# Node update of a two-layer graph network: ring of seven x blocks, counts inverted once, scalings on ScalarE, biases as bf16 rows, 14 blocks a turn

## What is computed

```python
feat_in, feat_out = h @ W_in.T + b_in, h @ W_out.T + b_out
a = concatenate(seg_mean(feat_in[src], dst), seg_mean(feat_out[dst], src))   # sums / max(count, 1)
gi, gh = a @ w_ih.T + b_ih, h @ w_hh.T + b_hh
r, z = sigmoid(i_r + h_r), sigmoid(i_z + h_z)
n = tanh(i_n + r * h_n)
x = layernorm(x + (1 - z) * n + z * h)                                        # layer 0, h = x
m = relu(concatenate(x[src], x[dst], bond) @ W1 + b1) @ W2 + b2
x = layernorm(x + x + segment_sum(m * sigmoid(bond @ Wa + ba), src))          # layer 1
```

## Time and profile before

| | us |
|---|---|
| three runs: median (lowest, highest) | 23,088.97 (23,025.80, 23,107.62) |
| profiled execution, its own time | 23,050.08 |
| its span | 23,048.5 |
| busy in it: PE / DVE / ACT / POOL | 12,864.9 / 8,520.6 / 3,852.9 / 9,828.0 |
| mean granted clock of PE | 0.681 of full speed |

### The profile page before, as it was taken

One profiled execution on the slowest core, in us unless ns is written; L12 is line 12 of the kernel. 1 busy time (PEld: TensorE's weight loads), 2 busy tenths in 40 slices (PEclk: granted clock), 3 DMA queues, 4 the chain that ended last, 5 costly groups with the idle time before them and its releaser, 6 DMA issues. The chain is left out here.

```text
span 23048.5 us, 371307 instructions
## 1 busy us (share of the span) xinstructions
PE 12864.9 (56%) x76034; PEld 9943.0 (43%) x76035; DVE 8520.6 (37%) x33126; ACT 3852.9 (17%) x9613; POOL 9828.0 (43%) x10418
## 2 busy tenths in 40 slices
PE   3444443444444444445555556777777777777773
PEld 2222223333333333335555544555555555555552
DVE  4333343332333333335545544333333333333333
ACT  0000001111111111100000002233333333333331
POOL 2444444444444444444444420344444444444440
PEclk9655556666666666667777778677677777777775
DMA  6222222222222222234444430111111131111131
GB/s 231 35 35 35 37 42 56 69 68 68 68 69 68 69 68 68 68 84 113 114 113 114 114 73 15 43 44 44 45 44 45 44 44 45 45 45 45 44 44 30
DMA packets 3234314, 1465.86 MB, mean 64 GB/s; under 512 B 2388398, under 2 KB 3029362, under 8 KB 3233775
## 3 DMA queue, kind: packets, MB, share of 16 engines
q1 hardware_dynamic: 2794486, 548.09, 12.8%
q0 software_dynamic: 386304, 796.93, 12.7%
q10 hardware_dynamic: 53492, 120.52, 1.5%
HBM read 1108.06 MB, written 467.75 MB: 68 GB/s over the span
## 5 line engine op out<-in xcount | busy, mean ns | idle before, releaser
L1522 POOL DMA_INDIRECT ring<-q_rows,small x3556 | 3369.8, 948 | 4597.3 <-ACT ring L1616 3609.8
L1562 PE MATMUL bank<-w,ring 64*128 64x129 f32 x7112 | 2334.8, 420 | 2074.4 <-DVE ring L1476 1183.7
L1562 PEld LDWEIGHTS bank<-w,ring 64*128 64x128 f32 x7112 | 1450.0, 254 | 2754.8 <-issue 1323.8
L876 PE MATMUL bank<-ident_b,ring 128*128 128x128 bf16 x3332 | 489.1, 298 | 3578.9 <-DVE ring L825 2241.1
L698 POOL DMA_INDIRECT ring<-in_x,small x1664 | 1572.5, 945 | 1926.7 <-DVE small L595 1276.3
L1080 POOL DMA_INDIRECT ring<-in_x,small x1664 | 1572.1, 945 | 1889.4 <-DVE small L1016 1244.4
L1475 DVE TENSOR_TENSOR ring<-bank,ring 128x256 f32<-128x256 f32 x1778 | 729.7, 419 | 4387.0 <-DMA edges_b<-ring,small 3651.7
L945 POOL DMA_INDIRECT edges_a<-ring,small x1664 | 1598.3, 961 | 1750.9 <-ACT ring L933 1300.5
L945 POOL DMA_INDIRECT edges_b<-ring,small x1664 | 1598.3, 961 | 1664.6 <-ACT ring L933 1212.7
L1100 PE MATMUL bank<-p,ring 128*128 128x129 f32 x8320 | 1482.8, 342 | 1463.7 <-issue 986.1
L1100 PEld LDWEIGHTS bank<-p,ring 128*128 128x128 f32 x8320 | 1387.3, 255 | 1505.3 <-issue 1505.2
(11 more groups left out here) (249 smaller groups left out, 23114.3 us busy)
## 6 DMA issues: line engine op xcount, KB each, us to landing
p<-edges_b SPq DMA_DIRECT2D x525, 262.0 KB
p<-edges_a SPq DMA_DIRECT2D x520, 262.0 KB
ring<-ids_by_dst SPq DMA_DIRECT2D x8360, 1.0 KB
ring<-bonds_by_dst SPq DMA_DIRECT2D x3328, 32.0 KB
bonds_by_dst<-in_bond ACTq DMA_DIRECT2D x5, 20625.0 KB
ring<-edges_a SPq DMA_DIRECT2D x1792, 33.0 KB
ring<-edges_b SPq DMA_DIRECT2D x1776, 33.0 KB
ring<-q_rows,small POOLq DMA_INDIRECT x3556
```

The source lines that it names most:

```text
L1522: pool.indirect_dma_start(out=gath[:, k, 0:D], out_offset=None, in_=c.q_dram, in_offset=bass.IndirectOffsetOnAxis(ap=gidx[g][:, k % HALF:k ...
L1562: nc.tensor.matmul(out, bond, c.weight(W_1C, D + 1, BOND), start=True, stop=False, skip_group_check=True)
```

## The change

Only `node_update` changes (its tiles now lie one after another in the same ring of 8,800 words). Loop one: `xs` has seven buffers, loaded seven blocks ahead; a turn of the loop is 14 blocks, with 6 turns and the seventh written out. max(count, 1) and its reciprocal are made for all 98 blocks in four instructions in the set-up; the two scalings a block go to ACT as ACTIVATE Copy with a scale per partition. The counts' square is replaced by a tile `has` (min(count, 1) of both sides and a one, three times), nine bf16 columns a block; a bf16 product with the identity turns it, and the biases are nine bf16 rows (three pieces each of three rows), laid on their partitions by six DMAs in the set-up. The gate arithmetic becomes keep = (1 + z) x, drop = (z - 1) n, y = keep - drop. PE now transposes b+1 ahead of the gates of b. Loop two: DVE normalises two blocks ahead, right behind `split`; ACT makes the first and the middle bf16 piece and copies q; b1 is added as three bf16 rows; PE transposes b+1 ahead of the products of b; q has a bank of its own. The order on POOL's queue stays.

```diff
+XSLOTS = 7
...
+    TURN, TURNS_N = 2 * XSLOTS, NB // (2 * XSLOTS)
...
+            with nc.allow_non_contiguous_dma(reason="one value per partition"):
+                sp.dma_start(col_in[:, 0:1], ins["b_in"]).then_inc(s_col, 16)
+                sp.dma_start(col_out[:, 1:2], ins["b_out"]).then_inc(s_col, 16)
+            for n in range(XSLOTS):
+                sp.dma_start(xs[n], c.x_pad[n * P:(n + 1) * P, :]).then_inc(s_in[n], 16)
...
+            for k, at in ((1, 0), (2, 1), (3, 2)):
+                sp.wait_ge(s_bias, 2 * k)
+                source, b1_source = ((piece[0], b1_piece[0]), (piece[1], b1_piece[1]), (piece[0], b1_piece[0]))[at]
+                sp.dma_start(rows9[3 * at:3 * at + 3, :], source).then_inc(s_biases[at], 16)
+                sp.dma_start(b1_rows[at:at + 1, :], b1_source).then_inc(s_biases[at], 16)
+            def reload(i, j):
+                b = i * TURN + j
                 sp.wait_ge(s_y, b + 1)
...
+                sp.dma_start(xs[j % XSLOTS], c.x_pad[bass.ds((b + XSLOTS) * P, P), :]).then_inc(s_in[j % XSLOTS], 16)
...
+            with sp.Fori(0, TURNS_N - 1) as i:
+                for j in range(TURN):
+                    reload(i, j)
+            for j in range(XSLOTS):
+                reload(TURNS_N - 1, j)
...
+            nc.vector.memset(has, 1.0).then_inc(s_zero, 1)
+            step.mark(nc.vector.tensor_scalar(rc_in, c.acc[:, :, D], 1.0, None, ALU.max))
+            step.mark(nc.vector.tensor_scalar(rc_out, c.sum_out[:, :, D], 1.0, None, ALU.max))
...
+            for k, sums in enumerate((c.acc, c.sum_out)):
+                nc.vector.tensor_scalar(has[:, :, :, k], sums[:, :, D:W].to_broadcast([P, NB + 1, 3]), 1.0, None,
+                                        ALU.min).then_inc(s_rc, 1)
+            step.wait()
+            nc.vector.reciprocal(rc_in, rc_in).then_inc(s_rc, 1)
+            nc.vector.reciprocal(rc_out, rc_out).then_inc(s_rc, 1)
...
+            step.mark(nc.vector.tensor_copy(bias[:, 0:3 * D], c.bank[2][0:3, 0:3 * D]))
+            step.link(nc.vector.tensor_copy(bias[:, 3 * D:4 * D], c.bank[3][0:3, 0:D]))
+            nc.vector.tensor_copy(piece[0], bias).then_inc(s_bias, 1)
...
+            step.mark(nc.vector.tensor_tensor(rest, bias, piece[0], ALU.subtract))
...
+            nc.vector.tensor_copy(piece[1], rest).then_inc(s_bias, 1)
...
+            dve.wait_ge(s_biases[0], 32)
+            nc.vector.tensor_tensor(piece[0], rest, piece[1], ALU.subtract).then_inc(s_bias, 1)
...
+            def gru(i, j):
+                n, b, x = j % 2, i * TURN + j, xs[j % XSLOTS]
+                y = flat(nodes[:, bass.ds(b, 1), :])
+                dve.wait_ge(s_sig, b + 1)
+                step.link(nc.vector.tensor_tensor(t1, cand[n][:, 0:D], rz[n][:, 0:D], ALU.mult))
+                nc.vector.tensor_tensor(t2, gates[n][:, 2 * D:3 * D], t1, ALU.add).then_inc(s_pre, 1)
+                step.mark(nc.vector.scalar_tensor_tensor(keep, rz[n][:, D:2 * D], 1.0, x, ALU.add, ALU.mult))
+                dve.wait_ge(s_tanh, b + 1)
+                step.link(nc.vector.scalar_tensor_tensor(drop, rz[n][:, D:2 * D], 1.0, t3, ALU.subtract, ALU.mult))
+                nc.vector.tensor_tensor(y, keep, drop, ALU.subtract).then_inc(s_y, 1)
+                dve.wait_ge(s_y, b + 1)
                 dve.sem_inc(s_go, 1)
-                step.mark(nc.vector.tensor_scalar(rc[:, 0:1], into[:, D:D + 1], 1.0, None, ALU.max))
-                step.link(nc.vector.tensor_scalar(rc[:, 1:2], out[:, D:D + 1], 1.0, None, ALU.max))
-                step.link(nc.vector.reciprocal(rc, rc))
-                nc.vector.tensor_scalar(mx[n][:, 0:W], into, rc[:, 0:1], None, ALU.mult).then_inc(s_m, 1)
-                nc.vector.tensor_scalar(m_out[n], out[:, 0:D], rc[:, 1:2], None, ALU.mult).then_inc(s_m, 1)
...
+                step.link(nc.vector.bn_stats(st, y))
+                dve.sem_inc(s_go, 1)
+                step.link(nc.vector.bn_aggr(st2, st))
+                nc.vector.tensor_copy(flat(mv[:, bass.ds(b, 1), :]), st2).then_inc(s_var, 1)
+            with dve.Fori(0, TURNS_N - 1) as i:
+                step.loop(i, 5 * TURN)
+                for j in range(TURN):
+                    gru(i, j)
+            step.end(TURNS_N - 1)
+            for j in range(TURN):
+                gru(TURNS_N - 1, j)
...
                 if not isinstance(turn, int):
                     dve.wait_ge(s_hout[n], 16 * turn)
-                dve.wait_ge(s_ht, b + 1)
-                dve.sem_inc(s_go, 1)
-                nc.vector.tensor_scalar(h1[n], y, mv[:, bass.ds(b, 1), 0], rstd[:, bass.ds(b, 1)],
-                                        ALU.subtract, ALU.mult).then_inc(s_h, 1)
-            normalise(0, 0, 0)
-            with dve.Fori(0, NB // 2) as i:
-                step.loop(i, 6)
+                    dve.wait_ge(s_ht, b - 1)
+                nc.vector.tensor_scalar(h1[n], flat(nodes[:, bass.ds(b, 1), :]), mv[:, bass.ds(b, 1), 0],
+                                        rstd[:, bass.ds(b, 1)], ALU.subtract, ALU.mult).then_inc(s_h, 1)
...
+            def split(b, n):
+                parts = flat(c.p3_b[:, bass.ds(b, 1), :])
+                dve.wait_ge(s_high, b + 1)
+                nc.vector.tensor_tensor(rem[n], c.bank[2 + n][:, 0:D], parts[:, 0:D], ALU.subtract).then_inc(s_rem, 1)
+            def lowest(b, n):
+                parts = flat(c.p3_b[:, bass.ds(b, 1), :])
+                dve.wait_ge(s_mid, b + 1)
+                nc.vector.tensor_tensor(parts[:, 2 * D:3 * D], rem[n], parts[:, D:2 * D], ALU.subtract).then_inc(s_low, 1)
+            for n in range(2):
+                normalise(n, n, 0)
+            with dve.Fori(0, NB // 2 - 1) as i:
                 for n in range(2):
-                    b = 2 * i + n
-                    normalise(b + 1, 1 - n, i + n)
...
-                    dve.wait_ge(s_pc, b + 3)
-                    nc.vector.tensor_copy(q[n], c.bank[2 + n][:, D:2 * D]).then_inc(s_qc, 1)
...
-                    step.link(nc.vector.tensor_copy(parts[:, 0:D], pf))
-                    step.link(nc.vector.tensor_tensor(rem, pf, parts[:, 0:D], ALU.subtract))
-                    step.link(nc.vector.tensor_copy(parts[:, D:2 * D], rem))
-                    nc.vector.tensor_tensor(parts[:, 2 * D:3 * D], rem, parts[:, D:2 * D], ALU.subtract).then_inc(s_split, 1)
-                    dve.wait_ge(s_split, b + 1)
...
+                    split(2 * i + n, n)
+                    normalise(2 * i + (n + 2), n, i + 1)
+                    lowest(2 * i + n, n)
...
-            def transposes(b, n):
-                pe.wait_ge(s_m, 3 * b + (3 + 6))
-                pe.wait_ge(s_tc, b + 1)
-                nc.tensor.transpose(c.bank[n][:, 0:P], mx[n][:, 0:D], c.ident)
-                nc.tensor.transpose(c.bank[n][:, P:2 * P], m_out[n], c.ident)
-                nc.tensor.transpose(c.bank[n][:, 2 * P:3 * P], mx[n][:, D:2 * D], c.ident)
...
+            def transposes(i, j):
+                n, b = j % 2, i * TURN + j
+                pe.wait_ge(s_mean, 2 * b + 2)
+                pe.wait_ge(s_in[j % XSLOTS], i * 32 + 16 * (j // XSLOTS + 1))
+                pe.wait_ge(s_tc, 2 * b + 2)
+                nc.tensor.transpose(turned[n][:, 0:P], m_in[n], c.ident)
+                nc.tensor.transpose(turned[n][:, P:2 * P], m_out[n], c.ident)
+                nc.tensor.transpose(turned[n][:, 2 * P:3 * P], xs[j % XSLOTS], c.ident)
+                nc.tensor.matmul(turned[n][0:9, 3 * P:4 * P], has[:, bass.ds(b, 1), :, :].rearrange("p o c k -> p (o c k)"),
+                                 c.ident_b[:, :], start=True, stop=True).then_inc(s_t, 1)
+            pe.sem_inc(s_tc, 4)
+            pe.sem_inc(s_pre, 2)
+            pe.wait_ge(s_folded, 2)
+            pe.wait_ge(s_bias, 2)
...
-                    nc.tensor.matmul(cand[n][:, 0:D], x_t, c.weight(W_HH + 2), start=True, stop=False)
-                    nc.tensor.matmul(cand[n][:, 0:D], has_t, bias[:, 3 * D:4 * D], start=False, stop=True).then_inc(s_gate, 1)
-                    transposes(b + 1, 1 - n)
...
+            for at in range(3):
...
+                pe.wait_ge(s_pre, b + 1)
+                pe.wait_ge(s_tc, 2 * b + 6)
+                in_t, out_t, x_t = (m_t[n][:, k * P:(k + 1) * P] for k in range(3))
+                nc.tensor.matmul(gates[n][:, 0:3 * D], in_t, c.weight(W_IH1, 3 * D), start=True, stop=False,
+                                 skip_group_check=True)
...
+                nc.tensor.matmul(gates[n][:, 0:3 * D], has_t[n], rows9[:, 0:3 * D], start=False, stop=True,
+                                 skip_group_check=True)
+                nc.tensor.matmul(cand[n][:, 0:D], x_t, c.weight(W_HH + 2), start=True, stop=False)
+                nc.tensor.matmul(cand[n][:, 0:D], has_t[n], rows9[:, 3 * D:4 * D], start=False,
+                                 stop=True).then_inc(s_gate, 1)
+            with pe.Fori(0, TURNS_N - 1) as i:
+                for j in range(TURN):
+                    transposes(i + (j + 1) // TURN, (j + 1) % TURN)
```

(62 more changed lines are left out.)

199 lines of the change are left out of this document (78 added, 121 removed).

## The result

The changed kernel takes 22,791.6 us (median of four runs, 22,769.4 to 22,824.9) against 23,098.3 for the kernel before (23,025.8 to 23,108.1): 307 us less, a ratio of 0.9875 with a 95% interval of 0.9851 to 0.9900. Forecast were 22,736 us and a gain of 353, with a range of 22,640 to 22,840. The profiled execution took 22,769.4 us, span 22,767.8.

What follows compares the result with a forecast made beforehand. It took loop one to be bound by a ring closed by the x load. Loop one -366 us (2.95 us a block, tables 9, set-up 2) and loop two +13 gave -353: 22,736 us, range 22,640 to 22,840.

Steps and rivals of the forecast that it cites:

- the second rival: Loop one held by sequencers (register waits, addresses or code fetches): 3.5 us a block or 40 us of fetches; chance 0.14.
- What bounds the kernel: Loop one before: a ring through all engines, closed by the load of x with only two buffers; 6.80 us a block.
- VectorE's chain, 2.80 us: Loop one after: VectorE's dependent operations sum to 2.68 us a block, plus 0.12 for register arithmetic of block numbers.
- TensorE, 2.7 us: Loop one, per block: f32 columns 1.95 us, bf16 bias products 0.25, transposes 0.5; 3.3 if bf16 gave nothing.
- Table loads: Loop one, ScalarE: one load a turn, 7 instead of 49, in the open at about 1.3 us each: 9 us.
- The fourth rival: Loop one: scaling needs another table than the sigmoid, two loads a block, 200 us above the forecast; chance 0.04.
- ScalarE's scalings free: Loop one: scalings moved to ScalarE make its ring 2.42 us, under VectorE's; no cost while 0.38 us of slack remains.
- Set-up +2: Before loop one: bias pieces laid out by DMA make the first sigmoid 2 us later (0 to 8).
- Loop two 3.33 us, +13: Loop two: from 3.2 to 3.33 us a block through a new POOL ring, 13 us slower over 98 blocks.
- Both rings named in the forecast: Loop two: one-block ring through split and normalise, 3.17 us; two-block ring through POOL's q and h, 3.33 a block.
- Clock: PE's granted clock: above 0.88 in loop one, 0.50 (the level of 1.2 GHz) in loop two.
- The third rival: Loop one: TensorE falls to 1.2 GHz, 5.4 us a block, 240 us above the forecast; chance 0.04.

Runs made afterwards that it cites:

- the pair of edits: Changed kernel with, in loop two, normalise ahead of split and h of the next block written ahead of q: update 599.5 us, 102.2 less.

## Why the forecast held, and where it was off

The time came out 56 us above the forecast and inside its range: the update gained 316 instead of 353, and the rest of the difference is scatter. But the mechanism of loop one came out otherwise than forecast: the forecast's own sign of being wrong, a sigmoid pace above 3.3 with VectorE idle behind PE, is what the trace shows (3.39; VectorE waits 72.5 us behind the sigmoid, and the sigmoid for PE). The 22,791.6 us lie where the second rival had put its time, 22,775 to 22,795, for another reason; that the range took this rival in is why it held, and that is luck as far as the mechanism goes. By the forecast's own steps:

- **What bounds the kernel** was right as far as shown: under the new order the pace is 10.1 us with two buffers of x and 3.39 with seven.
- **VectorE's chain, 2.80 us**: right, but hidden. In the variant with bf16 rows in 128 partitions t1 follows t1 after 2.85 us (L1249, 13394.20 and 13397.05), with VectorE waiting in it for the tanh alone and for its own results.
- **TensorE, 2.7 us**: the step that failed. The term measured 3.39, above the forecast's own bound of 3.3 for bf16 that gives nothing: 0.39 too little for the f32 columns, 0.17 for the bf16 biases, 0.13 for the transposes. The price of the bias products in f32 was taken from rows of a square of 128 rows, and the change makes them nine rows high. A product that differs in height from its neighbours costs itself and them: 0.55 us a block here (3.39 to 2.84), 0.73 with f32 rows. In full height the sum is 2.84, as forecast within 0.14. As PE became the bound, loop one took 3.45 a block, turns included, where 2.95 and 9 us for the tables were forecast: its sigmoids fell 43 us short of the forecast gain, and the items below give 6 of them back, which leaves the 37 that the update lacks. The rival of a loop held at 3.5 us had the size right, but for sequencers and code fetches, of which there is no sign: 30 and 11 packets on the two instruction queues after, 25 and 7 before.
- **Table loads**: seven in the forecast, twelve in fact, ten of them between the first and the last sigmoid; priced at 9 us, they cost 5.4, of which dropping one load of the two at each turn head gives back 2. As PE gets faster they cost more: in the variant with bf16 rows in 128 partitions PE waits 10.4 us for the scalings. The fourth rival (the copy wants another table than the sigmoid) is half true: it did so once a turn, at the branch, not in every block.
- **ScalarE's scalings free**: right but for those turn heads. Back on VectorE they cost 29.8 us.
- **Set-up +2**: +1.8; only the total was compared, not the parts that make it up. The last sigmoid to the first normalise, not priced, gave back 3.4.
- **Loop two 3.33 us, +13**: 3.33 and +10.8. Both rings named in the forecast were there, 3.17 and 3.33 by its sums, 3.3 both by the runs (the shorter sum had the bias product 0.10 too cheap). Its sign (normalise waiting for the DMA of h in most blocks) showed in one block only, because the one-block ring was as long. A right number with the wrong one of two equal rings in front; the pair of edits showed it, neither alone could.
- **Clock**: above 0.88 in loop one (0.98) and 0.50 in loop two, as forecast. The third rival, a fall to 1.2 GHz in loop one, did not come.

## What to carry to other kernels

When a product is made smaller, its price is not read from the rows of the larger one: keep a small contraction at the height of its neighbours by padding with zeros (44.0 us of the update here), or put the short products side by side (40.8 us). When a loop has several rings within a few per cent, opening one shows nothing; list them all and open them together. A reordering that looks ahead needs the buffers under it: with two buffers it made the loop slower here.

## What was not expected of the hardware

- A product with 3 or 9 rows between products of 128 rows holds up the weight load of its own and of the next product: 0.33 and 0.17 us in bf16, 0.33 and 0.55 in f32, at a granted clock of 2.4 GHz (0.98 over loop one). The same product with 128 rows, 119 of them zero, costs nothing of that. A change between f32 and bf16 alone costs these two products nothing.
- The stages outside the update took 22,066, some 21,000 or 14,080 us for the same code, from one execution to another, and the kernel before moved with them (23,098, 21,941 to 21,991, 15,112), while the update kept to 701.5 to 701.7 us. What sets this was not looked into. A ratio of totals says little of a stage unless the stage's own time stands beside it.
